# Summing the exponentials of two key tiles on GpSimd before the denominators of pooled attention, images two to four

## Chip, cores and metric
One core of one Trainium2 chip runs the whole program. The metric is the device time of one launch in microseconds (us), the median of several runs. Engines: TensorE (PE, weight loads PEld), VectorE (DVE), ScalarE (ACT), GpSimd (POOL), SyncE (SP, which issues all the transfers).

## What is computed
The input x is four images of 256 channels by 32 by 32. Two blocks are added to it one after the other, each on a group-normalised copy:

```
x = x + attention(gn(x))          # hifi: softmax in 2x2 windows, 4 heads; lofi: below, 4 heads
x = x + conv3x3(relu(gn(x) * mask(gn(x)))) + bias

# lofi, per image: 1024 queries, 256 keys (means of 2x2 windows), 4 heads of 32
attn = softmax(q @ k.T * SCALE)   # over the 256 keys
lo   = attn @ v ; lofi = lo @ l_proj_w + l_proj_b
```

In lofi every query has one softmax over 256 keys. Keys lie on the 128 partitions, so a head has two key tiles. The denominator of a query is the sum of its exponentials over both tiles, and the values are divided by it afterwards.

## The kernel before
Images are numbered 0 to 3 in the code (b); "image two" is b = 1. Each engine has its instructions in an order written by hand, tied by semaphores. For image b the work is a front (projections, maxima of the logits, window scores) and a rest (exponentials, values, output projections). The convolution of image b-1 is cut into 144 matmuls and fills the gaps of TensorE in both: `conv.more(n)` issues the next n of them, with the numbers of the tuples FRONT, REST, FRONT_1 and REST_1. The DVE, too, mixes image b's softmax with the tiles and results of image b-1's convolution (`conv_tiles` L791, `conv_low` L810, `conv_result` L880).

The parts that matter here, per image:
- Pooled scores, eight tiles of 128 keys by 1024 queries (head h has tiles 2h and 2h+1): two matmuls each on TensorE (L1231), then one exponential each on ScalarE (L563) into `probs`, counted by the semaphore st_exp. ScalarE does exponentials 0 and 1, then (b > 1) the high part of the convolution's second tiles (L557, `conv_high`), then 2 and 3, the copy `p_w` (L608), and later 4 to 7.
- Window softmax on the DVE (`window_maxima` L860, its second half `weights` L869 with L871 to L876), which TensorE's transposes L1392 wait for; ScalarE turns them into p_w, and the four value products follow (PE `values` L1396, DVE L986, then the sums L994 and L997). The sum of the first two products is GpSimd's (L427).
- GpSimd otherwise makes the window products (L379) and the sums of the mask (L362), and is idle from there to L427.
- Denominators: `by_head(2, ones)` (L1448), 16 matmuls of 32 columns by 512 queries that multiply probs by ones, two key tiles accumulated, four heads side by side in the array. Then `window_out` (L1435, two matmuls), then `by_head(0, lv)` (L1451), the 16 matmuls of the values, then convolution matmuls, then the wait for lnorm, and the output projection from q_w (L1459 to L1462). In the last image window_out stands ahead of the denominators.
- The DVE turns the denominators into a factor (two transposes L1013, reciprocal L1015, transpose L1016), adds the window output to the image (`residual(b, 0, 1)`, L898) and multiplies (L1021, lnorm). Then it makes the low half of the next image's normalised input (L706), adds the second output (`residual(b, 1, 2)`), and pools the next input for its keys (`pooling` L709 to L715). The key projection of the next front waits for the pooling.
- `qs`, `ks` hold queries and keys stacked by transfers; the exponentials live in `probs`.

Of the kernel before, what the change touches and what calls it, by code (L numbers as in the profile page):

```python
# [5 lines left out]
F32 = mybir.dt.float32  # L6
# [3 lines left out]
ALU = mybir.AluOpType  # L10
# [3 lines left out]
P = 128  # L14
B, C, H, W = 4, 256, 32, 32
KT = C // P
HW = H * W
# [7 lines left out]
MT = G // P  # L25
# [44 lines left out]


EARLY = 8
REST = (4, 3, 5, 3, 4, 8)


FRONT = (0, 11, 0, 0, 4, 3, 3, 3, 3, 3, 6, 10, 18)
# [1 line left out]


FRONT_1 = (0, 0, 0, 0, 0, 0, 0, 9, 5, 9, 7, 6, 0)  # L80
REST_1 = (1, 1, 2, 2, 2, 7)


WARM = (4, 1)
# [12 lines left out]
def wait_count(eng, sem, n):  # L97

    if not (isinstance(n, int) and n <= 0):
        eng.wait_ge(sem, n)  # L100
# [15 lines left out]
def build(nc, x, wqkv, whp, wlp, bh, bl, cw, cb, mw, filt, consts, selectors, out):  # L116
    with ExitStack() as ctx:
        def sb(name, shape, dt=F32):
            return ctx.enter_context(nc.sbuf_tensor(name, shape, dt))

        def sem(name):
            return ctx.enter_context(nc.semaphore(name))
# [16 lines left out]
        q_w = sb("q_w", [P, HW])  # L139
        k_w = sb("k_w", [P, HW])  # L140
        v_w = sb("v_w", [P, HW])
        qs = sb("qs", [P, HEADS, HW], F32R)
        ks = sb("ks", [P, HEADS, G], F32R)
        lv = sb("lv", [P, MT, P])
        probs_at = nc.sbuf_base
        probs = sb("probs", [P, LT, HW])
# [74 lines left out]
        pb_pe, pv_ready = sem("pb_pe"), sem("pv_ready")  # L221
        pv_pool, pv_dve = sem("pv_pool"), sem("pv_dve")
        st_pe, st_exp = sem("st_pe"), sem("st_exp")
        lden_pe, blocks_c, fold_c = sem("lden_pe"), sem("blocks_c"), sem("fold_c")
        lpv_pe, lnorm = sem("lpv_pe"), sem("lnorm")
        out_pe, y_ready = sem("out_pe"), sem("y_ready")
# [132 lines left out]
        def _(pool):  # L359
# [7 lines left out]
            def mask_sum(b, pooled):  # L367

                pool.wait_ge(mask_c, (b + 1) * N_MASK)
                pool.wait_ge(pool_c, pooled_by(pooled) * N_POOL)  # L370
                for k in range(KT):
                    mask_sum_of(k)

            def products(b):

                for j in range(NW):
                    if b == 0 and j == 2:
# [4 lines left out]
                        k_w[:, j * G:(j + 1) * G].unsqueeze(1).to_broadcast([P, NW, G]),  # L382
                        ALU.mult).then_inc(prod_ready, 1)

            def link(ins, wait):

                ins.then_inc(cw_pool, 1)
                if wait:
                    pool.wait_ge(cw_pool, wait)
# [21 lines left out]
            def step(b, first, last):  # L411
                if not first:
                    pool.wait_ge(proj_pe, b * 5 + 5)
                pool.wait_ge(qkv_sb, b * 3 + 2)
                wait_count(pool, mask_c, b * N_MASK)
                if b == 1:
                    mask_sum(0, 2)
                    pool.wait_ge(v_dve, KT)
                    pool.wait_ge(lv_pe, 1)
                products(b)  # L420
                if first:
                    inner_weights()
                else:
                    if b > 1:
                        mask_sum(b - 1, b + 1)
                    pool.wait_ge(pv_ready, b * NW + 2)
                    nc.gpsimd.tensor_tensor(pv[0], pv[0], pv[1], ALU.add).then_inc(pv_pool, 1)  # L427
            nc.gpsimd.memset(l_max[:], 0.0).then_inc(zeroed, 1)
            pool.wait_ge(zeroed, 1)
            nc.gpsimd.memset(ks[SC:SM].bitcast(F32), 1.0).then_inc(ones, 1)  # L430
# [15 lines left out]
        def _(act):  # L446
# [34 lines left out]
            def normalise(b):  # L481

                act.wait_ge(gn_c[0], (b + 1) * N_GN)
                act.wait_ge(xlo_ready, b * KT)
                act.wait_ge(pool_c, pooled_by(b) * N_POOL)
                act.wait_ge(pv_dve, b * 2)
                for k in range(KT):
                    scaled(b, k, xn).then_inc(xn_ready, 1)
                act.wait_ge(lpv_pe, b)
                for k in range(KT):  # L490
                    act.wait_ge(xn_ready, b * KT + k + 1)
                    nc.scalar.copy(xn_hi[:, k], xn[:, k]).then_inc(xhi_ready, 1)
# [9 lines left out]

            def projections(b, first):
                wait_count(act, lpv_pe, b)
                if not first:
                    sum_moments(b - 1, 0, probs[:, 3])
                act.wait_ge(proj_pe, b * 5 + 1)
                nc.scalar.copy(lq_hi, flat[0]).then_inc(lq_act, 1)
                if b == 1:
                    sum_moments(0, 1, probs[:, 3])  # L510
                if first:
                    act.wait_ge(cw_in, KT * 16)
                    weight_high(0, V_LEFT, 0)
                    weight_high(0, V_RIGHT, 2)
                act.wait_ge(proj_pe, b * 5 + 2)
                if first:
                    act.wait_ge(w_low, 2)
                    act.wait_ge(w_pooled, 1)
                nc.scalar.copy(lk_hi, slot[1][:, 0, 0:G]).then_inc(lk_act, 1)

                if b != 1:
                    values_of(slot[1])
                if b > 1:
                    sum_moments(b - 1, 1, probs[:, 3])
                wait_count(act, y_ready, b * KT)
                for i, (src, dst) in enumerate(((flat[2], q_w), (flat[0], k_w), (flat_cps if first else flat[1], v_w))):
                    act.wait_ge(proj_pe, b * 5 + i + 3)
                    nc.scalar.copy(dst[:], src).then_inc(qkv_sb, 1)
# [119 lines left out]
        def _(dve):  # L648
# [332 lines left out]
            def step(b, first, last):  # L981
# [23 lines left out]
                link = Chain(dve, blocks_c, N_BLOCKS, b)  # L1005
                blocks = v_w[:].rearrange("p (n c) -> p n c", c=HD)
                inv = s_den[:].rearrange("p n h -> p (n h)")
                if last:
                    residual(b, 0, 1)
                for i in range(2):  # L1010
                    h = slice(i * HALF, (i + 1) * HALF)
# [2 lines left out]
                link(ins)  # L1014
                link(nc.vector.reciprocal(inv, blocks[:, :, 0]))  # L1015
                link(nc.vector.transpose(blocks, inv.unsqueeze(2).to_broadcast([P, HW // HD, HD])))  # L1016
                if not last:
                    residual(b, 0, 1)
                dve.wait_ge(blocks_c, (b + 1) * N_BLOCKS)
                dve.wait_ge(lpv_pe, b + 1)  # L1020
# [90 lines left out]
        def _(pe):  # L1111
            def mm(dst, lhsT, rhs, start, stop):
                return nc.tensor.matmul(dst, lhsT, rhs, start=start, stop=stop)  # L1113
# [117 lines left out]
            def pooled_scores(b, i):  # L1231
# [4 lines left out]
                              True, True)  # L1236
                last.then_inc(st_pe, 1)

            def by_head(s, lhsT, ready):

                for half in range(2):
                    for t in range(MT):
                        for h in range(HEADS):
                            last = mm(slot[s][HD * h:HD * (h + 1), half], lhsT(t, h), probs[:, h * MT + t, halves(half)],
                                      t == 0, t == MT - 1)
                    if ready is lden_pe or half == 1:
                        last.then_inc(ready, 1)
# [15 lines left out]
            def front(b, conv, first=False):  # L1263
# [13 lines left out]
                    pe.wait_ge(y_ready, KT - 1)  # L1277
                    keys_of_sums()
                else:
                    if b == 2:  # L1280
                        conv.more(POOL_WAIT)
                    pe.wait_ge(pool_c, pooled_by(b + 1) * N_POOL)
                    if first:
                        pe.wait_ge(w_pooled, 1)
# [96 lines left out]
            def rest(b, first, last):  # L1381
# [63 lines left out]
                    window_out()  # L1445
                else:
                    group_means(b + 1, 0)
                by_head(2, lambda t, h: cst[:, C_ONE:C_ONE + HD], lden_pe)  # L1448
                if not last:
                    window_out()  # L1450
                by_head(0, lambda t, h: lv[:, t, HD * h:HD * (h + 1)], lpv_pe)  # L1451
                if last:
                    pe.wait_ge(y_ready, B * KT - 1)
                    group_means_of(0)
# [5 lines left out]
                for half in range(2):  # L1460
                    ins = mm(slot[2][:, half], w_out[:, 1], in_rows(q_w, half), True, True)
                ins.then_inc(out_pe, 1)  # L1462
                conv.more(OUT_MM - conv.at)
                return conv

            def step(b, first, last):
# [67 lines left out]
```

## Time and profile before
| | |
|---|---|
| median of 3 runs | 350.07 us (350.04 to 353.92) |
| span of the profiled execution, first to last instruction | 347.5 us |
| the profiled execution's own device time | not given apart from the span; median minus span is 2.6 us |
| busy share TensorE, DVE, ScalarE, GpSimd | 91%, 78%, 43%, 24% |
| mean granted TensorE clock | 0.979 |

Busy shares are means over the span. In a row of the timeline the columns are: start in us from the span's start, duration in us, engine, line, operation, output<-inputs, shape, how many instructions are merged in the row, and in brackets the idle time of the engine before it and what ended it. Duration includes the time in which an operation that has been started is held up.

### The profile page before, as it was taken

Reading aid. Unit: us, or ns where it says so; the run is one execution under the profiler, and the core shown is the slowest. Engines: PE = TensorE matmul, PEld = TensorE weight load, DVE = VectorE, ACT = ScalarE, POOL = GpSimd, SP = SyncE. Lnnn points to the kernel's source line nnn. Section 1 sums busy time; section 2 is a strip of 40 time slices with the busy share of each in tenths; the row PEclk is TensorE's granted clock in tenths of the full one; section 3 lists DMA queues with packets and bytes.
Section 4 is the critical chain, followed back from the end, with each engine's and each line's share of the span. In section 5 each row is a group of like instructions: output and inputs, shape, how many; then the busy total and the mean of one; then the engine's idle time right before and its main releaser. Section 6 shows DMA issues by size and latency. Waiting matters only on the chain.

```text
span 347.5 us, 4162 instructions
## 1 busy us (share of the span) xinstructions
PE 315.2 (91%) x1566; PEld 222.3 (64%) x1566; DVE 272.5 (78%) x488; ACT 148.8 (43%) x189; POOL 83.0 (24%) x46
## 2 busy tenths in 40 slices
PE   0879968999979999999799999999799999999995
PEld 0566344267866663688567744888388727877884
DVE  4996668769999586889989767799887847897572
ACT  2442548464490843554047855351165423031300
POOL 2088513440436020003910200008600200202000
PEclk9999968899989999999999999999999999999999
DMA  8779500009700000099011200197001000101002
GB/s 276 276 102 140 228 5 0 2 1 134 94 0 4 2 1 2 0 130 159 1 63 41 82 1 2 35 128 128 4 0 62 0 0 5 58 0 62 0 0 121
DMA packets 12068, 20.38 MB, mean 59 GB/s; under 512 B 2065, under 2 KB 8081, under 8 KB 11793
## 3 DMA queue, kind: packets, MB, share of 16 engines
q1 hardware_dynamic: 12048, 20.13, 28.2%
q8 instruction: 12, 0.20, 0.2%
q14 instruction: 8, 0.06, 0.1%
HBM read 7.93 MB, written 4.19 MB: 35 GB/s over the span
## 4 chain that ended last, share of the span: by engine, by line
PE 58%; DVE 23%; ACT 8%; issue 6%; POOL 3%; DMA 2%; SPq 0%; DVEq 0%; POOLq 0%
PE slot L1113 29%; PE cps L1145 15%; PE slot L1189 7%; DVE l_max L848 3%; PE cps L1113 3%; DVE mask L784 3%; PE cps L1189 2%; ACT probs L563 2%; POOL probs L379 2%; DVE v_lo L814 1%; DMA xy<-x 1%; PE slot L1392 1%; ACT xn_hi L452 1%; ACT p_w L608 1%; DVE xn L740 1%
## 5 line engine op out<-in xcount | busy, mean ns | idle before, releaser
L1145 PE MATMUL cps<-v_hi,cw_hi 128*128 128x512 f32 (+1 forms) x144 | 57.6, 400 | 3.5 <-DVE v_lo L814 2.9
L1145 PE MATMUL cps<-v_hi,cw_lo 128*128 128x512 f32 (+1 forms) x144 | 57.9, 402 | 0.0
L1145 PE MATMUL cps<-v_lo,cw_hi 128*128 128x512 f32 (+1 forms) x144 | 56.4, 392 | 0.0
L379 POOL TENSOR_TENSOR probs<-q_w,k_w 128x1024 f32<-128x1024 f32 x14 | 32.9, 2376 | 79.5 <-DVE rw L777 72.3
L848 DVE TENSOR_REDUCE l_max<-slot 128x4 f32<-128x1024 f32 x32 | 37.1, 1216 | 5.9 <-PE slot L1113 5.9
L563 ACT ACTIVATE probs<-slot 128x1024 f32<-128x1024 f32 x32 | 31.4, 1021 | 16.0 <-PE slot L1113 15.9
L1145 PEld LDWEIGHTS cps<-v_hi,cw_hi 128*128 128x128 f32 x144 | 27.4, 191 | 12.7 <-issue 5.2
L1145 PEld LDWEIGHTS cps<-v_hi,cw_lo 128*128 128x128 f32 x144 | 27.4, 190 | 7.4 <-issue 2.2
L1145 PEld LDWEIGHTS cps<-v_lo,cw_hi 128*128 128x128 f32 x144 | 27.4, 190 | 5.0
L362 POOL TENSOR_TENSOR mask<-rw 128x1024 f32<-128x1024 f32 x8 | 15.2, 1912 | 56.6 <-DVE rw L777 56.6
L1113 PE MATMUL slot<-xn_hi,w_hi 128*128 128x512 f32 (+1 forms) x68 | 27.3, 401 | 1.1 <-ACT xn_hi L452 1.1
L1113 PE MATMUL slot<-xn_hi,w_lo 128*128 128x512 f32 (+1 forms) x68 | 26.1, 383 | 0.0
L1113 PE MATMUL slot<-xn_lo,w_hi 128*128 128x512 f32 (+1 forms) x68 | 25.9, 381 | 0.0
L546 ACT ACTIVATE xn<-mask 128x1024 f32<-128x1024 f32 x8 | 8.5, 1061 | 39.0 <-DVE mask L784 39.0
L557 ACT ACTIVATE v_hi<-mask 128x1024 fp32r<-128x1024 f32 x16 | 16.8, 1058 | 18.0 <-DVE mask L806 10.6
L1113 PE MATMUL slot<-probs,cst 128*32 128x512 f32 x176 | 23.1, 638 | 0.0
L1113 PE MATMUL slot<-qs,ks 98*128 98x512 f32 x64 | 21.4, 428 | 1.7 <-DMA qs<-probs 1.7
L1113 PEld LDWEIGHTS slot<-ks,qs 96*128 96x128 f32 x128 | 18.2, 194 | 6.3 <-DVE l_max L848 3.8
L814 DVE SCALAR_TENSOR_TENSOR v_lo<-mask,v_hi 128x1024 fp32r<-128x1024 f32 x16 | 19.2, 1220 | 3.6 <-ACT v_hi L557 3.6
L1113 PE MATMUL slot<-ks,qs 96*128 96x256 f32 x128 | 20.3, 293 | 1.2 <-DVE l_max L848 0.8
L427 POOL TENSOR_TENSOR q_w<-q_w,k_w 128x1024 f32<-128x1024 f32 x3 | 7.3, 2419 | 56.8 <-DVE k_w L986 56.8
L532 ACT ACTIVATE xn<-xy,gn 128x1024 f32<-128x1024 f32 x8 | 9.6, 1239 | 17.2 <-DVE gn L679 17.2
(197 smaller groups left out, 635.0 us busy)
## 6 DMA issues: line engine op xcount, KB each, us to landing
xy<-x SPq DMA_DIRECT2D x8, 512.0 KB, 6.6
out<-xy SPq DMA_DIRECT2D x8, 512.0 KB, 2.6
qs<-probs SPq DMA_DIRECT2D x12, 256.0 KB, 5.8
qs<-probs SPq DMA_DIRECT2D x24, 128.0 KB, 8.3
raw_cw<-conv_w SPq DMA_DIRECT2D x2, 1152.0 KB, 6.4
ks<-probs SPq DMA_DIRECT2D x12, 128.0 KB, 6.9
probs<-h_qkv SPq DMA_DIRECT2D x2, 192.0 KB, 3.8
probs<-l_kv SPq DMA_DIRECT2D x2, 128.0 KB, 3.7
```

What stands on the lines that cost most here:

```text
L362: nc.gpsimd.tensor_tensor(mask[:, k].rearrange("p (h w) -> p h w", h=H), rw[:, k, 0].unsqueeze(2).to_broadcast([P, H, W]), rw[:, k, 1].uns ...
L379: nc.gpsimd.tensor_tensor(product(b, j).rearrange("p (n w) -> p n w", n=NW), q_w[:].rearrange("p (n w) -> p n w", n=NW), k_w[:, j * G:(j + ...
L532: nc.scalar.activation(xn[:, k], img(b, k), ACT.Identity, bias=gn[1][:, 6, k:k + 1], scale=gn[1][:, 5, k:k + 1]).then_inc(yn_ready, 1)
L546: nc.scalar.activation(xn[:, k], mask[:, k], ACT.Relu).then_inc(relu, 1)
L557: nc.scalar.activation(v_hi[:, k, 2 * phase:2 * phase + 2].rearrange("p a b -> p (a b)"), mask[:, k], ACT.Copy, scale=TILE_SCALE[phase]).t ...
L563: nc.scalar.activation(probs[:, i], flat[score_slot(b, i)], ACT.Exp, scale=SCALE / NW)\
L784: nc.vector.scalar_tensor_tensor(mask[:, k], mask[:, k], -1.0, xn[:, k], ALU.max, ALU.mult).then_inc(masked, 1)
L814: nc.vector.scalar_tensor_tensor(v_lo[:, k, part].rearrange("p a b -> p (a b)"), mask[:, k], TILE_SCALE[phase], v_hi[:, k, part].rearrange ...
L848: nc.vector.tensor_reduce(l_max[:, bass.ds(n, HEADS, step=NB)], flat[LA_SLOT[n]].rearrange("p (h m) -> p h m", h=HEADS), AX_X, ALU.max, ne ...
L1113: return nc.tensor.matmul(dst, lhsT, rhs, start=start, stop=stop)
L1145: ins = nc.tensor.matmul(cps[:, pos % 2, y0 * WT:y1 * WT], (cw_hi, cw_hi, cw_lo)[part][:, k, pos, dy + 1, o * P:(o + 1) * P], (v_hi, v_lo, ...
L1189: ins = nc.tensor.matmul(last_bank(o, pos)[:, y0 * WT:y1 * WT], (cw_hi, cw_hi, cw_lo)[part][:, k, pos, dy + 1, o * P:(o + 1) * P], (v_hi, ...
```

## The change
A tensor `key_sums` (4 heads by 1024, float32) is laid over `qs`. On GpSimd, for b of 1 to 3, four additions are put in: key_sums[h] = probs[2h] + probs[2h+1]; those of heads 0 and 1 ahead of L427, those of heads 2 and 3 behind it, each waiting for its two exponentials. TensorE's denominators of these images are 8 matmuls over key_sums in place of 16, and they come behind the values, with a wait for all four sums. ScalarE gets two waits on the sums (it overwrites what they read). On the DVE the window residual moves ahead of the denominator transposes. The convolution matmuls behind the denominators are 9 more (17, 16 for b = 1); `conv.more` at the end of rest is 9 fewer, and the 8 ahead of the key projection of b = 2 go.

```diff
-REST = (4, 3, 5, 3, 4, 8)
+REST = (4, 3, 5, 3, 4, 17)
-REST_1 = (1, 1, 2, 2, 2, 7)
+REST_1 = (1, 1, 2, 2, 2, 16)
...
+        key_sums = nc.alloc_sbuf_tensor_at("key_sums", [P, HEADS, HW], F32, offset=qs_at)
...
+            def key_sum(b, heads):
+
+                for h in heads:
+                    pool.wait_ge(st_exp, b * LT + (h + 1) * MT)
+                    nc.gpsimd.tensor_tensor(key_sums[:, h], probs[:, h * MT], probs[:, h * MT + 1],
+                                            ALU.add).then_inc(ksum, 1)
...
                     if b > 1:
                         mask_sum(b - 1, b + 1)
+                    key_sum(b, range(HEADS // 2))
                     pool.wait_ge(pv_ready, b * NW + 2)
                     nc.gpsimd.tensor_tensor(pv[0], pv[0], pv[1], ALU.add).then_inc(pv_pool, 1)
+                    key_sum(b, range(HEADS // 2, HEADS))
...
                 act.wait_ge(lpv_pe, b)
+                wait_count(act, ksum, (b - 1) * HEADS)
...
             def projections(b, first):
                 wait_count(act, lpv_pe, b)
+                wait_count(act, ksum, (b - 1) * HEADS)
...
-                if last:
+                if not first:
                     residual(b, 0, 1)
...
-                if not last:
+                if first:
                     residual(b, 0, 1)
...
+            def denominators(b):
+
+                pe.wait_ge(ksum, b * HEADS)
+                for half in range(2):
+                    for h in range(HEADS):
+                        last = mm(slot[2][HD * h:HD * (h + 1), half], cst[:, C_ONE:C_ONE + HD],
+                                  key_sums[:, h, halves(half)], True, True)
+                    last.then_inc(lden_pe, 1)
...
-                    if b == 2:
-                        conv.more(POOL_WAIT)
...
-                by_head(2, lambda t, h: cst[:, C_ONE:C_ONE + HD], lden_pe)
-                if not last:
+                if first:
+                    by_head(2, lambda t, h: cst[:, C_ONE:C_ONE + HD], lden_pe)
                     window_out()
                 by_head(0, lambda t, h: lv[:, t, HD * h:HD * (h + 1)], lpv_pe)
+                if not first:
+                    if not last:
+                        window_out()
+                    denominators(b)
...
-                conv.more(OUT_MM - conv.at)
+                conv.more(max(OUT_MM - conv.at, 0))
```

## Rows read from the trace of the kernel before
**Rows 1.** The page's part 4, chain of waits, share of the span by engine
```profile
PE 58%; DVE 23%; ACT 8%; issue 6%; POOL 3%; DMA 2%; SPq 0%; DVEq 0%; POOLq 0%
```
**Rows 2.** Timeline of image two, around exponentials 0 and 1
```profile
116.22 1.93 ACT L563 ACTIVATE probs<-slot 128x1024 f32<-128x1024 f32 x2
118.22 0.35 DVE L872 RECIPROCAL s_max<-s_den 128x32 f32<-128x32 f32 x1
118.61 0.29 DVE L873 TENSOR_TENSOR k_w<-k_w,s_max 128x128 f32<-128x128 f32 x1
...
119.54 1.09 PE L1392 MATMUL slot<-cst,k_w 128*128 128x128 f32 x8 [0.31 <-DVE k_w L876]
```
**Rows 3.** Timeline, places where GpSimd and DVE read SBUF together
```profile
22.54 4.42 POOL L340 TENSOR_TENSOR cw_lo<-raw_cw,cw_hi 128x768 fp32r<-128x768 f32 x2
22.63 5.14 DVE L340 TENSOR_TENSOR cw_lo<-raw_cw,cw_hi 128x768 fp32r<-128x768 f32 x2
...
300.63 1.92 POOL L362 TENSOR_TENSOR mask<-rw 128x1024 f32<-128x1024 f32 x1 [27.71 <-DVE rw L777]
301.31 1.26 DVE L666 TENSOR_TENSOR gn<-gn 128x1 f32<-128x1 f32 x1
```
**Rows 4.** Timeline, GpSimd, the one addition of this shape
```profile
195.87 2.42 POOL L427 TENSOR_TENSOR q_w<-q_w,k_w 128x1024 f32<-128x1024 f32 x1 [20.85 <-DVE k_w L986]
```
**Rows 5.** Timeline of image three and four, from exponentials 0 and 1 to the values
```profile
184.23 1.92 ACT L563 ACTIVATE probs<-slot 128x1024 f32<-128x1024 f32 x2
...
186.78 0.66 DVE L806 TENSOR_TENSOR mask<-xn 128x480 f32<-128x480 f32 x1
...
189.78 1.92 ACT L563 ACTIVATE probs<-slot 128x1024 f32<-128x1024 f32 x2
...
192.65 0.74 PE L1113 MATMUL slot<-p_w,sel 128*128 128x512 f32 x2 [0.30 <-ACT p_w L608]
...
264.02 1.92 ACT L563 ACTIVATE probs<-slot 128x1024 f32<-128x1024 f32 x2
...
266.21 1.02 ACT L608 CAST p_w<-slot 128x1024 fp32r<-128x1024 f32 x1 [0.28 <-PE slot L1392]
```
**Rows 6.** Timeline of image two, from the last exponentials to the output
```profile
128.46 1.23 DVE L997 TENSOR_TENSOR k_w<-q_w,xn 128x1024 f32<-128x1024 f32 x1
...
130.55 3.64 PE L1113 MATMUL slot<-probs,cst 128*32 128x512 f32 x32
...
130.86 0.16 DVE L666 TENSOR_TENSOR gn<-gn 128x2 f32<-128x2 f32 x1
...
134.12 1.98 PE L1113 MATMUL slot<-k_w,w_out 128*128 128x512 f32 x4
134.26 0.72 DVE L1013 STREAM_TRANSPOSE v_w<-slot 128x512 f32<-128x512 f32 x1 [0.65 <-PE slot L1113]
...
136.57 1.24 DVE L898 SCALAR_TENSOR_TENSOR xy<-slot,bias,xy 128x1024 f32<-128x1024 f32 x1
...
139.81 1.23 DVE L1021 TENSOR_TENSOR q_w<-slot,v_w 128x1024 f32<-128x1024 f32 x1 [2.00 <-PE slot L1113]
```
**Rows 7.** Chain of waits in order of time, start and duration, eight convolution matmuls
```profile
146.00 1.80 PE cps L1145 x8
```
**Rows 8.** Timeline, key projections of images three and four, and the pooling before
```profile
147.61 0.30 PEld L1113 LDWEIGHTS slot<-p_w,w_hi 128*128 128x128 f32 x2 [0.23 <-DVE p_w L715]
...
220.05 0.69 DVE L715 TENSOR_TENSOR p_w<-mask,p_w 128x512 fp32r<-128x512 f32 x1
...
221.95 0.40 PE L1113 MATMUL slot<-p_w,w_hi 128*128 128x256 f32 x2
```
**Rows 9.** Timeline of the last image, DVE ahead of its row sums
```profile
293.78 0.69 DVE L891 SCALAR_TENSOR_TENSOR xy<-cps,xy 128x512 f32<-128x512 f32 x1 [0.92 <-PE cps L1145]
```
**Rows 10.** Busy time by stretch: PE, PEld, DVE, ACT, POOL, granted clock, DMA
```profile
97.60:99.60 2.00, 0.00 (x0) 0.00 (x0) 2.00 (x4) 1.85 (x3) 0.00 (x0) 1.00 0.00 0
101.00:103.00 2.00, 2.00 (x8) 1.68 (x7) 2.00 (x3) 1.91 (x5) 2.00 (x1) 0.51 0.00 0
```

More of the change, by code:

```diff
@@ L141, in build @@
         v_w = sb("v_w", [P, HW])
+        qs_at = nc.sbuf_base
         qs = sb("qs", [P, HEADS, HW], F32R)
         ks = sb("ks", [P, HEADS, G], F32R)
+        key_sums = nc.alloc_sbuf_tensor_at("key_sums", [P, HEADS, HW], F32, offset=qs_at)
         lv = sb("lv", [P, MT, P])
@@ L223, in build @@
         st_pe, st_exp = sem("st_pe"), sem("st_exp")
+        ksum = sem("ksum")
         lden_pe, blocks_c, fold_c = sem("lden_pe"), sem("blocks_c"), sem("fold_c")
```

## The prediction
> **What bounds the kernel now.** I read the page's chain of waits first. It runs through TensorE for 58% and the DVE for 23% [rows 1], so neither alone is the bound and the answer lies in the stage. Then I read the timelines of the three stages that the change touches. In image two TensorE's transposes start at 119.54, after 0.31 us idle, on the end of the DVE's window softmax (L876) [rows 2]: the DVE is late here. In images three and four the window values start behind ScalarE's copy p_w, which follows exponentials 2 and 3, which follow the second convolution tiles of the DVE [rows 5]. From there to the last exponential TensorE is full. After it, TensorE goes through denominators, window output and values, and the DVE's product waits 2.00 us for the values [rows 6]. Behind the product the DVE is the late one again: the key projection of image three waits 0.23 us for the DVE's pooling [rows 8].
>
> **What the change takes away.** 16 denominator matmuls take 134.12 - 130.55 = 3.57 us (the row's 32 records are two per matmul) [rows 6]. Eight take 1.79 us. So TensorE has 1.8 us less to do in each of three images, 5.4 us in all. The nine convolution matmuls are only moved: 1.80 us for eight is 0.225 each, 2.0 us for nine [rows 7].
>
> **The tail of image two, step by step.** Values start at 130.55 and end at 134.12, window output ends at 136.1 (the 1.98 us of the old one), denominators end at 137.9. The DVE's second transpose starts 0.14 us after the last denominator (134.26 against 134.12), and from it to the next long operation are 136.57 - 134.26 = 2.31 us (transposes, reciprocal) [rows 6]. Now the residual stands in front: it starts near 136.2 and takes 1.2, so the first transpose goes at 137.4, the second at 138.1, and the product at 140.5. Before it was 139.81. The DVE chain is 0.7 us later, though TensorE is 1.8 us earlier: the stall on the values has gone, and the denominators, which used to lie under window output and values, are late in its place. Price +0.7. ScalarE's casts come earlier and hide.
>
> TensorE needs for its 16 convolution matmuls until 141.5 and the product ends at 141.7, so it stands 0.3 us. Pooling ends 0.7 later, and with the eight matmuls ahead of it gone TensorE idles some 2 us before the key projection. That idle time is cover lost, not price; the price is the 0.7.
>
> **The tail of image three** is the same, but the key projection starts at 221.95, 1.2 us after pooling ended at 220.74 [rows 8]: TensorE was late there. Pooling now ends about 0.6 later, at 221.3, and TensorE, relieved, is ready. So -0.6.
>
> **The tail of image four.** Product and second residual come about 0.4 late, but the DVE's wait of 0.92 us for the convolution's last position [rows 9] goes, since these matmuls now run ahead. Its row sums begin some 0.6 earlier. -0.6.
>
> **The four additions on GpSimd.** The one addition of this shape takes 2.42 us [rows 4]. Four are 9.7 us per image, on an engine that is idle. The denominators wait for the last. In image two exponential 7 ended before the old denominators began at 130.55, the last sum follows by 133 to 134.5, the denominators want it at 136.1: hidden. The same holds in the other two.
>
> **What the additions hold up.** This is the term that decides. When GpSimd runs a two-input operation, a DVE operation with both tensors in SBUF doesn't start working until it ends: L666, normally 0.16 us [rows 6], took 1.26 and ended at 302.57, where GpSimd's L362 ended at 302.55 [rows 3]. Two pairs of the same subtraction, started together, alternate: GpSimd 4.42 us for two, DVE 5.14 [rows 3], that is one waits for the whole of the other, in turns.
>
> The Trainium skill (SBUF — State Buffer, section Who interferes with whom) has a rule that speaks against this change: a DVE instruction with two SBUF inputs and a GpSimd one that reads SBUF exclude each other for the whole instruction, and whichever is issued first goes first. By that rule the additions cost 8.7 us plus 0.3, as below. If the two only shared the port and slowed each other in part, a 0.29 us operation would lose little more than its own length, and the total would be near rival 2. The trace agrees with the rule: 1.26 us for 0.16.
>
> Image two: exponentials 0 and 1 end at 118.15. The sum of head 0 starts near 118.24, before L873 (118.61), which has two SBUF inputs. L873 waits until 120.65 and ends at 120.9. Then it is GpSimd's turn: head 1 (exponentials 2 and 3 end 1.9 us or so after 0 and 1) runs 120.9 to 123.3, and L876 waits for it: 123.6 in place of 119.5 [rows 2]. TensorE, ScalarE's p_w and the values follow at once. +4.1. If the cast L875 and L876 slipped in between the sums it would be 2.1; the upper end is both sums, 2 x 2.4 = 4.8.
>
> Image three: exponentials 0 and 1 end at 186.15, just as the DVE enters L805 and L806 of the second convolution tiles. L806 (186.78, two SBUF inputs) waits for a sum: 2.4 us. ScalarE's L557, exponentials 2 and 3 behind it (189.78), p_w, and the values at 192.65 shift with it [rows 5]: +2.5. The sum of head 1 starts then at 194.3, where the DVE works from PSUM. Bounds: 0 if the DVE keeps its turn throughout, 4.8 for two sums.
>
> Image four: the same collision; exponentials 2 and 3 move from 264.02 to 266.45 and p_w behind them from 266.21 to 268.3 (it was waiting for TensorE, so 0.3 is absorbed) [rows 5]. +2.1, same bounds.
>
> The sums of heads 2 and 3 meet L997 (128.46) and the small normalisation operations from L666 at 130.86 to the first transpose (134.26 - 0.65 - 0.72 = 132.9) [rows 6]. Head 2 runs 128.4 to 130.8, L997 until 132.0, head 3 until 134.4, then the 2.0 us of small operations until 136.4; the residual could start at 136.2. +0.3 in image two, nothing in the others, where the tail is more relaxed.
>
> **TensorE's clock.** TensorE will stand for about 4 us in image two, 3 in image three, 2 in image four. Before, after 2.00 us without a matmul, the granted clock was 0.51 from 101 to 103, that is 1.2 of 2.4 GHz, against 1.00 in the stretch of the pause [rows 10]. Two such microseconds cost one where TensorE is full. The values and exponentials behind these pauses are such places. Bounds 0 and about 1.7 per pause; I take 1.0 for one fall, nearest to the row.
>
> **Sum.** 4.1 + 0.7 + 0.3 (image two), 2.5 - 0.6 (three), 2.1 - 0.6 (four) = 8.5, and 1.0 for the clock: +9.5. Against the profiled execution: span 347.5 to 357.0. The median lies 2.57 above that span, hence 359.6. 2% of 350.07, 7.0 us, is about what a measurement of this kernel can tell from no change; 357.1 is the line.
>
> **Rivals.**
> 1. The lock costs less (0.17). The DVE's unbroken run of tile operations keeps its turn and the additions slip into gaps, where they hold up only L814 or one softmax step. 2.1 + 1.0 + 2.5 - 0.6 - 0.6 = +4.4: 354.5. For it: no row shows a GpSimd operation that has to wait for a stream without semaphores in it. Against: L340 alternates.
> 2. No collision at all, not slower (0.12): GpSimd starts too late for L873 and L806, or the hold-up falls where the DVE has slack. One mechanism, the place is L873 at 118.61; it decides if the sum of head 0 starts more than 0.37 us after the exponential. Then the tails alone count: +0.7 - 0.6 - 0.6 = -0.5: 349.6. Against it: the DVE answered TensorE within 0.14 us (134.12 to 134.26) [rows 6], and GpSimd has nothing else to do.
> 3. TensorE is the bound everywhere, and the 1.8 us come out in full (0.03): 350.07 - 5.4 = 344.7. Against it: TensorE waits for the DVE [rows 2, 8].
> 4. The clock falls at each of the pauses (0.10): 8.5 + 3 x 1.7 = +13.6: 363.7.
> The forecast has 0.58; its own range is 356.5 to 363. The range over the cases is 352.5 to 364, which leaves out rivals 2 and 3. Slower by over 2%: nine tenths of the forecast, all of rival 4, a little of rival 1: 0.66. Within 2%: 0.33. Faster by over 2% (under 343.1): 0.01.
>
> **What would show it.** In the profile after: L873 and L876 of image two with durations near 2 us each; L805 or L806 near 3 us in two of their eight instances; TensorE's idle time before L1392 in image two near 4 us, and before the first matmul on p_w in images three and four some 2.5 us; the product L1021 no longer waiting for the values, with TensorE waiting for it or level; the key projection of image three about 0.7 later behind its product, with idle before it. Wrong would be: L873 at 0.29 us, or GpSimd's additions stretched beyond 2.42 us while the DVE's stay short.

## The result and the profile after

The changed kernel takes 363.01 us (360.72 to 363.20), the kernel before 351.81 us in the same comparison (350.04 to 353.92): ratio 1.036, 95% interval 1.031 to 1.041. The medians are 11.2 us apart, while the ratio stands for some 12.6 us (3.6% of 350), because ratios are taken over the faster executions alone and medians over all, and the kernel before has some executions that are slower by over 1% at a lower granted clock. The forecast was 359.6, slower by 9.5.

The page of the kernel after, its part 2 (granted clock in 40 slices) and part 4 (chain of waits by engine):

```profile
span 361.1 us, 4080 instructions
...
PEclk9999988999989699989899899999899899999998
...
PE 53%; DVE 29%; ACT 8%; issue 5%; DMA 3%; SPq 0%; DVEq 0%; ACTq 0%
```

Against [rows 1] the chain has moved from TensorE (58% to 53%) to the DVE (23% to 29%), though TensorE's work became less. The mean granted clock fell from 0.979 to 0.950.

The unchanged stretch ahead of image two's exponentials took 1.2 us less in this execution (exponential 0 at 115.04 against 116.22) and varies from one execution to the next: in the runs below it ends between 112.6 and 118.1. So stages are compared here by their distance from that exponential, and whole kernels by their medians. From exponential 0 to the last instruction are 246.1 us (361.1 - 115.04) against 231.3 (347.5 - 116.22): 14.8 more, of which the front gives back 1.2. The time outside the span gives back another 0.8: it was 1.8 in this execution (362.9 - 361.1), where the forecast took 2.57.

**Image two, window softmax.** Timeline of the kernel after, GpSimd, DVE, ScalarE and TensorE, the lines that answer to [rows 2]:

```profile
115.04 1.93 ACT L577 ACTIVATE probs<-slot 128x1024 f32<-128x1024 f32 x2
117.05 4.70 POOL L392 TENSOR_TENSOR key_sums<-probs 128x1024 f32<-128x1024 f32 x2 [8.00 <-ACT probs L577]
117.44 2.11 DVE L887 TENSOR_TENSOR k_w<-k_w,s_max 128x128 f32<-128x128 f32 x1
119.59 2.25 DVE L889 CAST k_w<-k_w 128x128 fp32r<-128x128 f32 x1
121.87 0.29 DVE L890 TENSOR_TENSOR k_w<-k_w 128x128 f32<-128x128 f32 x1
...
125.29 1.22 PE L1127 MATMUL slot<-p_w,sel 128*128 128x512 f32 x2 [0.28 <-ACT p_w L622]
```

L887 (before L873) takes 2.11 us for 0.29, L889 2.25, each ending where an addition of GpSimd ends (the two additions are 117.05 to 121.75). L890 comes 6.83 us after exponential 0 where it came 2.97 us after.

**Images three and four, convolution tiles.** The same for the lines that answer to [rows 5], image three first:

```profile
193.23 0.65 DVE L819 TENSOR_TENSOR mask<-xn 128x480 f32<-128x480 f32 x1
193.24 3.61 POOL L392 TENSOR_TENSOR key_sums<-probs 128x1024 f32<-128x1024 f32 x1 [12.22 <-ACT probs L577]
...
193.79 0.66 DVE L820 TENSOR_TENSOR mask<-xn 128x480 f32<-128x480 f32 x1
194.36 0.19 DVE L817 TENSOR_SCALAR mask<-xn 128x32 f32<-128x32 f32 x1
194.47 2.43 DVE L818 COPY mask<-xn 128x32 f32<-128x32 f32 x1
...
198.07 1.06 ACT L571 ACTIVATE v_hi<-mask 128x1024 fp32r<-128x1024 f32 x1 [2.46 <-DVE mask L820]
199.03 1.92 ACT L577 ACTIVATE probs<-slot 128x1024 f32<-128x1024 f32 x2
...
201.91 0.96 PE L1127 MATMUL slot<-p_w,sel 128*128 128x512 f32 x2 [1.80 <-ACT p_w L622]
...
272.61 2.44 DVE L818 COPY mask<-xn 128x32 f32<-128x32 f32 x1
```

Here the addition is the one that waits first: it stands 1.2 us (3.61 for 2.4) while the DVE goes through L819 and L820. Then a copy of 32 columns, 0.19 us else, is held for the whole addition. TensorE waits 1.80 us for p_w where it waited 0.30.

**TensorE's clock.** Busy time by stretch (length, PE, PEld, DVE, ACT, POOL, granted clock, DMA), first behind the pause in image two, then behind the start of the values of images three and four, one stretch ahead of image three's window scores, and one behind its key projection:

```profile
119.00:125.00 6.00, 2.78 (x10) 2.10 (x10) 3.09 (x3) 0.87 (x2) 2.75 (x2) 0.61 0.00 0
202.00:206.00 4.00, 4.00 (x11) 3.22 (x12) 2.23 (x2) 3.26 (x7) 1.40 (x1) 0.57 0.40 131
280.00:284.00 4.00, 3.95 (x11) 3.15 (x12) 2.37 (x3) 0.00 (x0) 1.54 (x1) 0.59 0.00 0
178.00:180.00 2.00, 2.00 (x7) 1.34 (x6) 1.80 (x4) 0.00 (x0) 2.00 (x2) 0.59 0.00 0
154.00:158.00 4.00, 4.00 (x15) 3.29 (x14) 2.58 (x4) 2.73 (x6) 0.00 (x0) 0.57 1.08 124
```

The granted clock of 0.57 to 0.61 says that most of each is at 1.2 GHz, the lower of the two levels, and in all of them TensorE is full or an engine waits for it. In the kernel before the stretches that answer to the first three (120 to 124, 193 to 197 and 265 to 269 us) are granted 1.00, and from exponential 0 to the last matmul nothing is below full clock. In the changed kernel there is one more such stretch, in image four, 0.61 from 256 to 260 us.

The falls at 178 and at 256 us need no change. TensorE stands there for the DVE's maxima in every kernel, and what follows differs between executions in which TensorE's work is the same. Around that pause of image three, first the kernel before (TensorE stands 1.54 us), then the run with a memset told below (1.53 us):

```profile
170.00:172.00 2.00, 0.55 (x3) 0.51 (x4) 1.58 (x3) 0.00 (x0) 2.00 (x2) 1.00 0.00 0
...
169.00:172.00 3.00, 3.00 (x14) 1.02 (x16) 2.90 (x2) 0.00 (x0) 2.52 (x2) 0.50 0.17 36
```

From the key projection to exponential 0 of image three are 36.60 us without this fall (184.23 - 147.63, kernel before) and 37.32 with it (181.46 - 144.14, memset).

**The tails.** TensorE and DVE behind the last exponentials of image two, then the key projections of images three and four, the lines that answer to [rows 6, 8]:

```profile
134.74 3.64 PE L1127 MATMUL slot<-probs,lv 128*32 128x512 f32 x32
138.31 1.98 PE L1127 MATMUL slot<-k_w,w_out 128*128 128x512 f32 x4
140.23 1.92 PE L1127 MATMUL slot<-key_sums,cst 128*32 128x512 f32 x16
140.34 1.28 DVE L912 SCALAR_TENSOR_TENSOR xy<-slot,bias,xy 128x1024 f32<-128x1024 f32 x1
...
144.64 1.23 DVE L1035 TENSOR_TENSOR q_w<-slot,v_w 128x1024 f32<-128x1024 f32 x1
...
152.43 0.30 PEld L1127 LDWEIGHTS slot<-p_w,w_hi 128*128 128x128 f32 x2 [2.15 <-DVE p_w L729]
...
232.02 0.50 PE L1127 MATMUL slot<-p_w,w_hi 128*128 128x256 f32 x2 [0.80 <-DVE p_w L729]
```

The eight denominator matmuls take half of the sixteen, behind the values. The product has no wait in brackets any more: it comes off the DVE's own chain, 9.90 us after the values began, where it came 9.26 after the old denominators began (139.81 - 130.55).

### The profile page after: what moved, and what is told of

It is laid out like the page before. It is cut to its first block, busy times and chain, and to the rows that moved or that the text cites. A ratio compares the mean times of both kernels' runs of the same rounds, so it can differ in the third digit from the quotient of the medians.

```text
span 361.1 us, 4080 instructions
## 1 busy us (share of the span) xinstructions
PE 320.2 (89%) x1518; PEld 226.1 (63%) x1518; DVE 285.3 (79%) x488; ACT 148.5 (41%) x189; POOL 115.0 (32%) x58
## 4 chain that ended last, share of the span: by engine, by line
PE 53%; DVE 29%; ACT 8%; issue 5%; DMA 3%; SPq 0%; DVEq 0%; ACTq 0%
PE slot L1127 25%; PE cps L1159 15%; PE slot L1203 7%; DVE l_max L862 6%; ACT probs L577 3%; PE cps L1203 2%; PE cps L1127 2%; DMA ks<-probs 2%; DVE xy L912 2%; DVE v_lo L828 2%; DVE xn_lo L720 2%; DVE mask L818 1%; ACT p_w L622 1%; DVE mask L726 1%; DMA xy<-x 1%
## 5 line engine op out<-in xcount | busy, mean ns | idle before, releaser
L1159 PE MATMUL cps<-v_hi,cw_hi 128*128 128x512 f32 (+1 forms) x144 | 59.3, 412 | 5.5 <-DVE v_lo L828 3.2
L1159 PE MATMUL cps<-v_hi,cw_lo 128*128 128x512 f32 (+1 forms) x144 | 59.6, 414 | 0.0
L1159 PE MATMUL cps<-v_lo,cw_hi 128*128 128x512 f32 (+1 forms) x144 | 57.9, 402 | 0.0
L392 POOL TENSOR_TENSOR key_sums<-probs 128x1024 f32<-128x1024 f32 x12 | 32.1, 2680 | 47.6 <-ACT probs L577 47.4
L1159 PEld LDWEIGHTS cps<-v_hi,cw_hi 128*128 128x128 f32 x144 | 28.2, 196 | 16.2 <-issue 6.3
L1159 PEld LDWEIGHTS cps<-v_hi,cw_lo 128*128 128x128 f32 x144 | 28.3, 197 | 7.1 <-issue 1.3
L1159 PEld LDWEIGHTS cps<-v_lo,cw_hi 128*128 128x128 f32 x144 | 28.3, 196 | 5.0
L1127 PE MATMUL slot<-xn_hi,w_hi 128*128 128x512 f32 (+1 forms) x68 | 28.2, 415 | 0.3 <-DVE xn_lo L720 0.3
L828 DVE SCALAR_TENSOR_TENSOR v_lo<-mask,v_hi 128x1024 fp32r<-128x1024 f32 x16 | 19.2, 1220 | 3.8 <-ACT v_hi L571 3.8
L1127 PE MATMUL slot<-qs,ks 98*128 98x512 f32 x64 | 20.5, 412 | 1.7 <-DMA qs<-probs 1.7
L343 POOL TENSOR_TENSOR cw_lo<-raw_cw,cw_hi 128x768 fp32r<-128x768 f32 x6 | 11.7, 1978 | 14.4 <-DVE gn L693 8.1
```

Source lines behind the costliest of these rows:

```text
L343: return engine.tensor_tensor(cw_lo[:, k, pos], taps[k][:, tap], cw_hi[:, k, pos].bitcast(F32), ALU.subtract)
L392: nc.gpsimd.tensor_tensor(key_sums[:, h], probs[:, h * MT], probs[:, h * MT + 1], ALU.add).then_inc(ksum, 1)
L828: nc.vector.scalar_tensor_tensor(v_lo[:, k, part].rearrange("p a b -> p (a b)"), mask[:, k], TILE_SCALE[phase], v_hi[:, k, part].rearrange ...
L1159: ins = nc.tensor.matmul(cps[:, pos % 2, y0 * WT:y1 * WT], (cw_hi, cw_hi, cw_lo)[part][:, k, pos, dy + 1, o * P:(o + 1) * P], (v_hi, v_lo, ...
```

## The experiments

The medians of the kernel before were 350.26 us beside four of the runs (additions moved, additions alone, new order alone, additions of heads 0 and 1) and 350.36 beside four others (heads 2 and 3, half the size, memset, matmuls of no use). Line numbers shift by a few from kernel to kernel: the DVE's first subtraction of a window softmax is L873 before, L887 after, and L885 to L889 in most of the runs; the operation and the tile name it.

**The change with its first two additions moved in time.**

```diff
+                    pool.wait_ge(v_dve, b * POS)
+                    pool.wait_ge(soft_c, (b + 1) * N_SOFT)
                     key_sum(b, range(HEADS // 2))
```

> The changed kernel, but GpSimd's additions of heads 0 and 1 wait for the end of the DVE's window softmax and for the last low tiles of the older convolution, so that they run where the DVE has no operation with two SBUF inputs. Theory (the additions hold up the DVE, and TensorE's pauses behind them let its clock fall): both terms go, only the tails are left, 349 to 352 us; L887 and L889 of image two are at 0.2 to 0.3 us again, no stretch behind the window softmax is at half clock. Rival (the new order of the denominators and the moved convolution matmuls cost most of it): 359 us or more.

Measured: 351.17 us, ratio 1.001 (0.996 to 1.005). Two waits on an idle engine take back the loss, as far as these runs can tell. The DVE in image two:

```profile
118.58 0.29 DVE L889 TENSOR_TENSOR k_w<-k_w,s_max 128x128 f32<-128x128 f32 x1
118.90 0.23 DVE L891 CAST k_w<-k_w 128x128 fp32r<-128x128 f32 x1
```

The same work, the same new order of the tail, and no hold-up. So the rival that blames the order of the denominators and the moved convolution matmuls falls. The text expected no half clock behind the window softmax, and there is none (119 to 125 us are granted 1.00); exponentials 2 and 3 of images three and four follow 0 and 1 after 5.55 us, as before.

**The additions alone, in the kernel before.** The sums are made and read by nobody; the denominators are the old ones.

```diff
+                    key_sum(b, range(HEADS // 2))
                     pool.wait_ge(pv_ready, b * NW + 2)
                     nc.gpsimd.tensor_tensor(pv[0], pv[0], pv[1], ALU.add).then_inc(pv_pool, 1)
+                    key_sum(b, range(HEADS // 2, HEADS))
```

> The kernel before, with the four additions per image on GpSimd at the places of the change, their result read by nobody; denominators, order and convolution as before. Theory: nearly the whole loss is here, 358 to 363 us, with two DVE operations of image two held up by some 2 us each. Rival (order of the tail): at most 352 us.

Measured: 359.95 us, ratio 1.029 (1.023 to 1.036), that is some 10 of the 12.6 us, with nothing of the order changed. In image two L887 takes 2.12 and L889 2.24 us. In image three of this trace the collision took another form than in the change:

```profile
190.79 4.80 POOL L392 TENSOR_TENSOR key_sums<-probs 128x1024 f32<-128x1024 f32 x1 [11.21 <-ACT probs L577]
...
193.85 6.16 DVE L828 SCALAR_TENSOR_TENSOR v_lo<-mask,v_hi 128x1024 fp32r<-128x1024 f32 x2
```

The addition waited through both pairs of subtractions (4.80 us for 2.4), exponentials 2 and 3 were on time, and the two operations L828 took 6.16 us for 2.35. TensorE then waited 1.44 us for the DVE's first product, and its clock stayed full. The last exponential of the image began 19.60 us after its exponential 0 (208.39 - 188.79), against 17.87 before and 21.70 in the change.

**Only the additions of heads 0 and 1; only those of heads 2 and 3.** Each is the edit above with one of its two lines.

> The kernel before with the additions of heads 0 and 1 alone, unused. Theory: these two are what hurts (4.1 + 2.5 + 2.1 us and the clock behind the pauses), 357 to 362 us. Rival (all four hurt alike, by taking GpSimd and the port for 9.7 us per image): about half of the loss of the four, 353 to 355 us.

> The kernel before with the additions of heads 2 and 3 alone, unused. They meet the last window addition and the small normalisation operations of the DVE. Theory: these stand in front of slack, except in image two, 350 to 353 us. Rival (all four hurt alike): 353 to 356 us.

Measured: 356.37 us, ratio 1.022 (1.015 to 1.028), for heads 0 and 1; 351.75 us, 1.003 (0.998 to 1.008), for heads 2 and 3. GpSimd does the same work in both, 4.8 us per image. What counts is what the DVE does meanwhile. In the second run the DVE is held up as well, but ahead of slack:

```profile
129.67 3.41 DVE L1010 TENSOR_TENSOR k_w<-q_w,xn 128x1024 f32<-128x1024 f32 x1
...
133.78 1.56 DVE L679 TENSOR_TENSOR gn<-gn 128x2 f32<-128x2 f32 x1
```

After 2.2 and 1.4 us of hold-up the key projection of image three comes 0.2 us later behind exponential 0 of image two than before (31.62 for 31.41). The interval on the whole time ends at 0.8%, 2.8 us. The median for heads 0 and 1 is 0.6 below the range that was written down.

**A write without a read.** A memset of the same columns in place of each addition of heads 0 and 1.

```diff
-                    nc.gpsimd.tensor_tensor(key_sums[:, h], probs[:, h * MT], probs[:, h * MT + 1],
-                                            ALU.add).then_inc(ksum, 1)
+                    nc.gpsimd.memset(key_sums[:, h], 0.0).then_inc(ksum, 1)
```

> The kernel before with a memset by GpSimd of the same 1024 columns in place of each addition of heads 0 and 1: the same waits, the same place, a write of the same size, but no SBUF input. Theory (the second read path is what is contended): L886, the two-input operation of image two, is at 0.29 us; a copy or cast of the DVE may still be held up for the length of one memset; 350 to 352 us. Rival (any GpSimd work beside the DVE, or the wait itself, costs): 355 us or more.

Measured: 350.41 us, ratio 1.001 (0.996 to 1.006). GpSimd and DVE in image two:

```profile
114.63 0.96 POOL L392 MEMSET key_sums<- 128x1024 f32 x1 [7.98 <-ACT probs L575]
...
115.03 0.29 DVE L885 TENSOR_TENSOR k_w<-k_w,s_max 128x128 f32<-128x128 f32 x1
115.36 0.30 DVE L887 CAST k_w<-k_w 128x128 fp32r<-128x128 f32 x1
```

L885 begins and ends inside the memset at its usual 0.29 us. The cast behind it takes 0.30 for 0.23 and ends just after the memset. A memset is also shorter, 0.96 against 2.4 us, so the time alone would not tell much; the row does. It is GpSimd's reading that a DVE operation with two SBUF inputs waits for. In images three and four, too, no operation of the DVE is held up beside a memset (L826 takes 2.35 us for two).

**Half the size.** The additions of heads 0 and 1 over 512 queries, unused.

```diff
-                    nc.gpsimd.tensor_tensor(key_sums[:, h], probs[:, h * MT], probs[:, h * MT + 1],
+                    nc.gpsimd.tensor_tensor(key_sums[:, h, 0:HALF], probs[:, h * MT, 0:HALF], probs[:, h * MT + 1, 0:HALF],
```

> As the kernel before with the additions of heads 0 and 1, unused, but over 512 of the 1024 queries. Theory (a DVE operation with two SBUF inputs waits for the rest of the GpSimd operation): each hold-up halves to some 1.2 us, pauses of TensorE stay near 2 us and its clock falls less; from the start of image two's exponentials to the end some 4 to 6 us more than before, where the whole additions gave 10.2; 352 to 355 us. Rival (a fixed cost per GpSimd operation): as with the whole additions, 356 us.

Measured: 352.41 us, ratio 1.005 (1.001 to 1.009), less than half of what the whole additions cost. In image two and in image three:

```profile
117.49 1.28 POOL L392 TENSOR_TENSOR key_sums<-probs 128x512 f32<-128x512 f32 x1 [8.01 <-ACT probs L576]
```
```profile
117.88 1.04 DVE L886 TENSOR_TENSOR k_w<-k_w,s_max 128x128 f32<-128x128 f32 x1
118.95 0.23 DVE L888 CAST k_w<-k_w 128x128 fp32r<-128x128 f32 x1
...
188.14 0.20 DVE L817 COPY mask<-xn 128x32 f32<-128x32 f32 x1
...
189.98 2.85 DVE L827 SCALAR_TENSOR_TENSOR v_lo<-mask,v_hi 128x1024 fp32r<-128x1024 f32 x2
```

The first hold-up shrinks with the addition (L886 ends with it, at 118.92 against 118.77). The second one isn't there, since a short addition is over before exponential 3 is. In image three the addition for head 0, at 186.91, took 3.70 us: it stood while the DVE went through four back-to-back subtractions, and cost the DVE only 0.5 us at L827. Image four shows the same. From exponential 0 of image two to the end this execution takes 2.2 us more than before (349.0 - 115.49 = 233.5), where 4 to 6 were expected, though the median is inside its range. So this run is no clean scale of size; with the additions alone above it shows that who gets in between two back-to-back DVE operations is not fixed.

**The new order alone.** The change without additions; the denominators are 16 matmuls over the exponentials again, behind the values.

```diff
-                pe.wait_ge(ksum, b * HEADS)
...
+                    for t in range(MT):
+                        for h in range(HEADS):
+                            last = mm(slot[2][HD * h:HD * (h + 1), half], cst[:, C_ONE:C_ONE + HD],
+                                      probs[:, h * MT + t, halves(half)], t == 0, t == MT - 1)
```

> The changed kernel without the additions: the denominators are again 16 matmuls over the exponentials, behind the values, all else as in the change. Theory: no hold-up and no fallen clock; the DVE's product comes 0.7 + 1.8 = 2.5 us later in image two, 1.2 in image three and some 1 to 2 in image four, 352 to 356 us. Rival: 359 us or more.

Measured: 355.51 us, ratio 1.017 (1.010 to 1.024). In image two:

```profile
131.40 3.64 PE L1125 MATMUL slot<-probs,lv 128*32 128x512 f32 x32
134.97 1.98 PE L1125 MATMUL slot<-k_w,w_out 128*128 128x512 f32 x4
136.88 3.64 PE L1125 MATMUL slot<-probs,cst 128*32 128x512 f32 x32
```
```profile
140.59 0.72 DVE L1025 STREAM_TRANSPOSE v_w<-slot 128x512 f32<-128x512 f32 x1 [1.00 <-PE slot L1125]
...
143.01 1.23 DVE L1033 TENSOR_TENSOR q_w<-slot,v_w 128x1024 f32<-128x1024 f32 x1
```

The product comes 11.61 us after TensorE starts its tail, 2.35 later than before, where 2.5 was expected. Placing the denominators last costs; making them eight pays this back, nearly to the microsecond. That is about all that the change's saving on TensorE is worth in image two.

**Matmuls of no use in the pauses.** The changed kernel, with matmuls into free banks where TensorE stands.

```diff
+                    if b == 1:
+                        pe.wait_ge(soft_c, b * N_SOFT + SOFT_READ)
+                        warm(slot[2], 6)
                     turned_weights()
                     conv.more(fill[2])
+                    if b > 1:
+                        pe.wait_ge(st_exp, b * LT + 3)
+                        warm(slot[0], 3)
...
+                        warm(slot[1], 3 if b == 2 else 1)
                     pe.wait_ge(pool_c, pooled_by(b + 1) * N_POOL)
```

> The changed kernel with matmuls of no use in TensorE's pauses (six ahead of the window transposes of image two, three ahead of the first window values of images three and four, three and one ahead of the key projections of images three and four), into banks that are free there. Theory (about 4 us of the loss is TensorE's clock after the pauses): the stretches behind the pauses are at full clock and the time falls by 2.5 to 5 us, to 358 to 360.5 us. Rival (the pauses alone, or TensorE's share of work, are the cost): 362 us or more.

Measured: 358.40 us, ratio 1.024 (1.016 to 1.032), against the 363.01 of the change: 4.6 us come back from adding work. Stretches that answer to the first three above:

```profile
122.00:128.00 6.00, 5.01 (x22) 3.00 (x21) 3.18 (x3) 1.16 (x2) 2.83 (x2) 1.00 0.00 0
198.00:204.00 6.00, 5.92 (x24) 4.13 (x23) 6.00 (x4) 4.84 (x9) 2.58 (x1) 1.00 0.29 90
277.00:283.00 6.00, 6.00 (x28) 4.89 (x27) 5.50 (x6) 0.97 (x1) 3.48 (x2) 1.00 0.01 3
```

From exponential 0 of image two to the last matmul the clock is full everywhere. The 4.6 us of the medians are no measure of its price, though. In the two traces, exponential 0 to the end takes 8.0 us less (356.2 - 118.11 = 238.1 against 246.1), while the front, where nothing differs, takes 3.1 more. What can be compared cleanly are images two and four, where the hold-ups are those of the change (L887 2.13 and L889 2.26 us; L818 2.45):

- image two, from exponential 0 to the last four: 14.05 us, against 15.55 in the change and 10.18 before. The clock costs 1.5, the hold-up 3.9.
- image four, from exponential 0 to the last: 20.25 us, against 21.68 and 18.30. The clock costs 1.4, the hold-up 1.9.

In image three the collision has the other form here, that of the additions alone: L828 takes 6.15 us for two, exponentials 2 and 3 are on time, and the last exponential comes after 19.57 us, as there. So image three doesn't tell the clock's share. From exponential 0 on this execution is 6.8 us longer than the kernel before, against 8.5 for the prediction's steps without the clock.

**Two versions built on this.** The first keeps the moved additions and takes the new tail in images three and four only; image two keeps its old denominators, order and fills. The second is the moved additions with useless matmuls ahead of the two key projections.

> The gated version of the first run with the new tail in images three and four alone; image two has the old denominators, order and fills. Theory: the tail costs the DVE's 0.7 us in image two only, and is worth 0.6 in each of images three and four, so about 1.2 us less than the kernel before, 348.5 to 350 us against its 350.3. Rival (the tails are worth nothing once the sums are out of the way): the same time as before within 0.3 us.

> The gated version of the first run with three matmuls of no use ahead of the key projection of image three and one ahead of that of image four. Theory: the gated version still loses some 1 us to TensorE's slow clock behind that pause, which the DVE's group normalisation waits for; 349 to 350.5 us. Rival (the pause costs nothing in time, as the prediction had it): equal to the gated version, 351 us.

Measured beside 351.32 us for the kernel before: 347.78 us, ratio 0.992 (0.987 to 0.996), for the first, and 349.34 us, 0.996 (0.992 to 1.001), for the second. The first beats both kernels, and its median lies 0.7 below the range written down. Its key projection of image four:

```profile
221.16 0.50 PE L1131 MATMUL slot<-p_w,w_hi 128*128 128x256 f32 x2 [0.80 <-DVE p_w L733]
```

It comes 104.98 us after exponential 0 of image two (116.18), where it came 105.73 after (221.95 - 116.22) [rows 2, 8]: 0.75 earlier, the 0.6 of the tail of image three. From exponential 0 to the end it is 230.1 us against 231.3, the 1.2 that the theory gave; what else lies between the medians, 3.5 us apart, is not placed by these traces. The second isn't told apart from the kernel before, and its ratio overlaps that of the moved additions without these matmuls (1.001): once the hold-up is away, filling the pauses has no gain that these runs show. The moved additions had nothing to give back there: TensorE stands 1.72 us ahead of image three's key projection, and the clock behind it is full (149 to 153 us, 1.00). So the second version's time is in the range written down, but the loss that the text gave as its reason isn't in the trace of the moved additions.

## Why the prediction came out as it did

Distances from exponential 0 of image two, after minus before, growing from stage to stage:

| up to | predicted growth | measured growth | of it ascribed to the clock |
|---|---|---|---|
| image two, end of window softmax (L876, L890) | +4.1 | +3.9 | |
| its first values | 0 | +0.9 | 0.9 |
| its last four exponentials | 0 | +0.6 | 0.6 |
| key projection of image three | +1.0 | +0.6 | |
| first values of image three | +2.5 | +4.4 | 2.2 |
| last exponential of image three | 0 | +1.6 | 1.6 |
| key projection of image four | -0.6 | -0.8 | |
| first values of image four | +2.1 | +2.7 | 0.9 |
| last exponential of image four | 0 | +1.5 | 1.5 |
| end | -0.6 | -0.7 | |
| clock, not placed | +1.0 | | |
| sum | +9.5 | +14.8 | 7.7 |

The sum is taken from unrounded figures. The median missed by 3.4 us and not by 5.3 only because the front and the time outside the span gave back 1.2 and 0.8: that is luck.

**What held.** The exclusive turn between GpSimd and DVE, as the term that decides. In image two both lengths were right, and one of the two places: the second hold-up fell on the cast L889, one operation ahead of L890, which the prediction had named (as L876). In images three and four the shifts were 2.25 us (exponential 0 to the first values, 10.67 for 8.42) and 1.85 for 2.5 and 2.1, though the copy L818 paid them and not L806. TensorE stood 4.17, 1.80 and 1.80 us, where 4, 3 and 2 were predicted. The three tails came out within 0.4 us each, the residual's place in front of the transposes included. GpSimd's last sum was indeed hidden. Without the clock the steps add up to 7.1 us against 8.5. The sign and the order of size were right.

**What failed is the size of one term: the clock.** The prediction wrote 1.0 us, "one fall", for it, though it had listed three pauses and a bound of 1.7 each (no row gives that bound). The clock fell behind all three. The stretches that start at these pauses grew by 0.9 and 0.6 in image two, 1.6 in image three and 1.5 in image four: 4.6 us. For images two and four the run with useless matmuls shows it, 1.5 and 1.4 given back with the same hold-ups. For image three it is argued, from a granted clock of 0.57 and from the likeness to image four. Rival 4, with 0.10, had this mechanism and is what happened; that its 363.7 is so near to 363.01 is partly luck, since it had neither the falls below nor what the front gave back.

**A second step that failed:** "That idle time is cover lost, not price." Ahead of image three's key projection TensorE stood 1.72 us (its weight loads 2.15), and 154 to 158 us are at a granted 0.57. From there to exponential 0 of image three are 38.81 us (191.24 - 152.43) for 36.60: 2.2 more. 0.7 of it is the price of the fall at 178 us, which comes without the change too. The other 1.5 go with the fall behind the pause. The DVE's group normalisation waits there for a tiny matmul behind the projections; its two waits on TensorE, the first with no counterpart before, the second 0.75 there:

```profile
162.05 0.16 DVE L707 COPY gn<-slot 128x4 f32<-128x4 f32 x1 [1.00 <-PE slot L1127]
...
186.28 0.29 DVE L880 TENSOR_REDUCE s_max<-slot 128x32 f32<-128x128 f32 x1 [1.76 <-PE slot L1382]
```

The second is 1.47 in the run with a memset as well, so most of what it is longer by belongs to the fall at 178 us. The pause does not always cost: the moved version and the new order alone stood 1.72 and 1.71 us at this place with full clock behind. In the run with useless matmuls, which fills it, the stretch is back at 36.63 us. What decides whether the clock falls there is not shown.

**What is not the change's.** Of image four's +2.7, 0.9 go with the fall at 256 us. The runs with a memset, with half the size and with heads 2 and 3 alone have the same stretch at 37.2 to 37.3 us, as the change has (37.37), and the kernel before happens to have 36.52. So some 1.6 of the 14.8 us are a difference between two executions.

**Rivals 1 to 3.** Rival 1 is half right in its mechanism: the DVE did keep its turn through L819 and L820 in image three, but the addition only came later, and the DVE paid at L818. In image three of the additions alone and of the run with useless matmuls the DVE kept its turn through all four subtractions and paid at L828, the place that rival 1 names (L814 there), and this was cheaper: 1.7 us by the last exponential, against 1.9 to 2.2 for the other form without the clock. Rival 2 needed GpSimd to start late; it started 0.08 us after the exponentials' end (117.05 against 116.97). Rival 3, TensorE as the bound, falls with the run of the new order alone.

## What to carry to other kernels

An idle engine isn't free to use when its reads hold up the one that is late: before GpSimd gets a two-input operation, list what the DVE runs in those microseconds, and if an operation with two SBUF inputs or a copy there is on the chain, delay GpSimd by a wait until the DVE reads PSUM. A hold-up of 2 us on another engine is priced with what it does to TensorE's clock: price each pause (here 1.4 to 1.6 us), not one. Compare two traces stage by stage before a difference of medians is given to a cause: here the falls that come anyway moved single stages by 0.7 us, and the front moved by up to 5.5. And a matmul that is saved counts only where TensorE is late; a stage that ends in the DVE's chain pays for the order in which it gets its inputs.

## What was not expected of the hardware

- A copy of 32 columns and a cast of 128, each with one SBUF input, waited for GpSimd's addition just as two-input operations do (2.43 and 2.25 us for 0.19 and 0.23). A reciprocal and a transpose of the DVE beside an operation of GpSimd that reads SBUF (L340, 64.02 to 67.68) in the kernel before did not lengthen: 0.35 us at 65.45 and 1.25 at 65.84.
- GpSimd waits in the same way: an addition was held 1.2 us by two back-to-back DVE subtractions (3.61 us) in one execution and 2.4 us by four of them in another (4.80), and the one of half the length by four (3.70 for 1.28).
- TensorE fell to 1.2 GHz after standing 1.80 us in images three and four, with little work in the microseconds before (in image three it had stood 1.07 us from 191 and 0.47 us from 198). At one and the same pause of 1.7 us ahead of a key projection it fell in one kernel and not in two others. More work, of no use, made the kernel 4.6 us faster by the medians.
